# Router logits computed beside the attention products instead of from a transposed second LayerNorm, with a new order of work around them

## What is computed

```python
# x [8,256,512], ctx [8,256,512], mask [8,256], g_* are two scalars
h = layernorm(x)
p = softmax(where(mask, h @ ctx.T / sqrt(512), -1e30))
x = x + tanh(g_xattn) * where(any(mask), p @ ctx, 0)
h = layernorm(x)                                   # [2048, 512]
probs = softmax(h @ w_router.T)                    # 8 experts
top_v, top_i = top_k(probs, 2); top_v /= top_v.sum(-1)
# each row goes through its two experts (inner size 192)
y = sum_k top_v[k] * (silu(h @ gate_k.T) * (h @ up_k.T)) @ down_k.T
x = x + tanh(g_ffn) * y
```

## Time and profile before

| | us |
|---|---|
| median of 3 runs | 261.72 (261.54 to 262.96) |
| the profiled execution | 262.24 |
| its span, first to last instruction | 260.4 |
| PE busy | 242.4 (93%) |
| POOL busy | 166.8 (64%) |
| DVE busy | 164.5 (63%) |
| ACT busy | 146.8 (56%) |

### The profile page before, as it was taken

One profiled execution on the slowest core, in us unless ns is written; L12 is line 12 of the kernel. 1 busy time (PEld: TensorE's weight loads), 2 busy tenths in 40 slices (PEclk: granted clock), 3 DMA queues, 4 the chain that ended last, 5 costly groups with the idle time before them and its releaser, 6 DMA issues.

```text
span 260.4 us, 5397 instructions
## 1 busy us (share of the span) xinstructions
PE 242.4 (93%) x1484; PEld 207.7 (80%) x1484; DVE 164.5 (63%) x618; ACT 146.8 (56%) x307; POOL 166.8 (64%) x165
## 2 busy tenths in 40 slices
PE   1989999999999999998999999999999999999940
PEld 1867778877877778997989998999999999999920
DVE  4559989999997987977855354454454454454420
ACT  3487789988799663533535454454454454454430
POOL 1247889888989647384346654888688665767550
PEclk9999999999999999999999999999999999999985
DMA  6999999999995238376346845899889975987763
GB/s 195 392 390 401 397 371 379 381 345 334 365 399 194 86 102 253 112 149 126 43 59 147 155 91 123 135 166 159 150 162 157 170 137 87 166 156 135 109 79 44
DMA packets 25950, 52.08 MB, mean 200 GB/s; under 512 B 5248, under 2 KB 5376, under 8 KB 25920
## 3 DMA queue, kind: packets, MB, share of 16 engines
q0 software_dynamic: 8304, 19.83, 41.7%
q1 hardware_dynamic: 13008, 23.50, 25.3%
q10 hardware_dynamic: 4608, 8.39, 8.4%
HBM read 33.81 MB, written 17.89 MB: 199 GB/s over the span
## 4 chain that ended last, share of the span: by engine, by line
PE 82%; DMA 5%; issue 4%; SPq 2%; DVE 2%; POOL 2%; ACT 1%; another core or an unknown queue 0%; POOLq 0%; ACTq 0%
PE PO L1217 11%; PE S L1206 9%; PE S L1360 9%; PE S L1364 9%; PE S L1361 9%; PE A L1350 6%; PE PL L1234 5%; PE S L1371 3%; DMA WGl<-in_wgu 3%; PE A L1225 3%; PE A L1188 2%; DMA out<-YT,IXI 2%; PE PO L1384 1%; PE PO L1388 1%; PE A L1384 1%
## 5 line engine op out<-in xcount | busy, mean ns | idle before, releaser
L1360 PE MATMUL S<-WGh,XTh 128*128 x144 | 51.2, 355 | 0.1
L1361 PE MATMUL S<-WGl,XTh 128*128 x144 | 48.3, 336 | 0.0
L464 POOL DMA_INDIRECT XG<-x2s,IXG x30 | 29.5, 983 | 17.1 <-issue 6.8
L634 ACT ACTIVATE SG<-S 128x192 f32<-128x192 f32 x36 | 11.9, 331 | 48.6 <-PE S L1364 48.6
L531 POOL DMA_INDIRECT out<-YT,IXI x19 | 30.3, 1595 | 12.5 <-issue 7.7
L1092 DVE TENSOR_TENSOR H<-SG,S 128x192 f32<-128x192 f32 x36 | 12.7, 354 | 37.6 <-ACT SG L634 35.0
L422 POOL TENSOR_TENSOR rs<-mv,CS 128x1 f32<-128x1 f32 x32 | 19.4, 606 | 22.6 <-DVE mv L749 22.3
L1217 PE MATMUL PO<-CX,PT 128*128 128x512 f32 x64 | 31.3, 611 | 0.2 <-ACT PT L582 0.2
L1364 PE MATMUL S<-WGh,XTl 128*128 x144 | 30.9, 336 | 0.0
L1206 PE MATMUL S<-CT,XLT 128*128 128x256 f32 x128 | 30.3, 379 | 0.0
L1085 DVE TENSOR_TENSOR XTl<-A,XTh 128x512 fp32r<-128x512 f32 x37 | 25.5, 690 | 7.4 <-ACT XTh L627 6.5
(11 more groups left out here) (189 smaller groups left out, 556.1 us busy)
## 6 DMA issues: line engine op xcount, KB each, us to landing
WGl<-in_wgu SPq DMA_DIRECT2D x24, 256.0 KB, 6.4
X<-in_x SPq DMA_DIRECT2D x16, 256.0 KB, 5.7
CT<-in_ctxt SPq DMA_DIRECT2D x8, 512.0 KB, 6.5
CX<-in_ctxn SPq DMA_DIRECT2D x8, 512.0 KB, 6.0
out<-X ACTq DMA_DIRECT2D x16, 256.0 KB, 5.6
x2s<-Y ACTq DMA_DIRECT2D x16, 256.0 KB, 5.3
WD1l<-in_wd SPq DMA_DIRECT2D x8, 256.0 KB, 6.2
WS<-in_wd SPq DMA_DIRECT2D x6, 256.0 KB, 5.8
```

The costliest lines, as they stand in the source:

```text
L464: pool.indirect_dma_start(out=XG[:, xg(j), :], out_offset=None, in_=rows, in_offset=bass.IndirectOffsetOnAxis(ap=at, axis=0))\
L1360: pe.matmul(o, XTh[:, j % 2, c, :], WGh[:, bass.ds(e, 1), c, :], start=(c == 0), stop=False)
L1361: pe.matmul(o, XTh[:, j % 2, c, :], WGl[:, bass.ds(e, 1), c, :], start=False, stop=False)
```

## The change

The logits of the second LayerNorm are no longer computed from its transpose. With centred router weights WRc (each expert's weights less their mean over the channels, `centre`), the logit of a row is its second reciprocal root times (x + attention output) · WRc, and a common positive factor doesn't change which experts are largest. So:

- CT gets 8 more columns that hold WR (loaded with the context), and `score` runs over 264 columns (CC) instead of 256. The 8 columns are the logits of the centred input tile. `rowmax` copies them, scaled, to LG (one DVE instruction more per tile).
- `cw(b, c)`, new on PE, multiplies one half of a batch's transposed context with WRc into PL: 4 products of 8 columns per step, in place of `rt`. `cwe(b)`, new on ACT, copies the result behind the context in CX (now 520 columns wide), once per batch.
- `pv` runs in two pairs: 256 columns into PO and 264 into A1. PO and A1 are now one two-bank tensor PP. `x2` gets one more DVE instruction, which adds 1/sum times the 8 extra columns to LG; the old one reads both banks.
- `t2`, `rt` and `ev2` are gone, and with them Y2T.
- `top2` reads LG, and runs two steps sooner; `odd(b)`, new, takes the difference of the two largest logits times the reciprocal root (two DVE instructions per batch, where batches 5 to 7 had one), before `weigh`, which gets one exponential fewer. `slots`, `cum`, `tab` come one step sooner, `coefs` one later; `st1` stands behind `rowmax`.
- PE's order in a step: t1, score, tp, cw, pv instead of t1, tp, score, rt, pv, t2. `first_list` stands in step 15 ahead of `pv(13)`.
- The end of the attention and SIDES are written anew: `slots(4)` and `top2(6)` now lie inside the steps, `tp(15)` and `tx(0)` ahead of `pv(15)`, the first two gathers ahead of `second(13)`, `store_x2(15)` behind `silu(0)`. In tiles 0 to 3 PE has tab(4), cum(5); tab(5), cum(6); tab(6), cum(7).

```diff
-SIDES = [(4, 6, 6), (4, 5, 4), (2, 3, 5), (2, 2, 3), (2, 2, 2), (0, 2, 3), (2, 3, 5), (2, 1, 2)] + [(0, 0, 0)] * 31
+SIDES = [(3, 6, 6), (3, 5, 4), (2, 3, 3), (5, 1, 2), (0, 5, 0), (1, 4, 4), (0, 1, 3), (3, 3, 2), (0, 0, 0), (0, 0, 0)] + [(0, 0, 0)] * 29
...
+            def centre():
+                dve.wait_ge(s_gb, 1)
+                n = mark(dve.reduce_sum(wm[:, :], PC[:, 16:48].rearrange("p (k e) -> p e k", e=E), AX.X))
+                yield
+                need(n)
+                dve.scalar_tensor_tensor(out=WRc[:, :, :], in0=wm[:, :].unsqueeze(1).to_broadcast([128, KC, E]),
+                                         scalar=-1.0 / D, in1=WR[:, :, :], op0=ALU.mult, op1=ALU.add).then_inc(s_wrc, 1)
+                yield
...
                 n = mark(dve.reduce_max(nmx[:, k:k + 1], SC[k % 2][:, 0:S], AX.X, negate=True))
                 yield
+                logit[k] = mark(dve.tensor_scalar(LG[:, k, :], SC[k % 2][:, S:CC], 1.0 / SCALE, None, ALU.mult))
+                yield
...
-                dve.scalar_tensor_tensor(out=xt, in0=PO[:, :], scalar=rinv[:, k:k + 1], in1=xt,
+                need(logit[k])
+                logit[k] = mark(dve.scalar_tensor_tensor(out=LG[:, k, :], in0=A1[:, S:CC], scalar=rinv[:, k:k + 1],
+                                                         in1=LG[:, k, :], op0=ALU.mult, op1=ALU.add))
+                dve.scalar_tensor_tensor(out=xh, in0=PP[:, :, 0:S], scalar=rinv[:, k:k + 1], in1=xh,
                                          op0=ALU.mult, op1=ALU.add).then_inc(s_x2, 1)
...
+            def odd(b):
+                dve.wait_ge(s_rs2, 2 * b + 2)
+                dve.wait_ge(s_lc, b + 1)
+                if b:
+                    dve.wait_ge(s_e2, b)
+                for i in range(2):
+                    n = dve.scalar_tensor_tensor(out=dd[:, i, :], in0=mx[:, i, 1:2], scalar=mx[:, i, 0:1],
+                                                 in1=rs2[:, 2 * b + i:2 * b + i + 1], op0=ALU.subtract, op1=ALU.mult)
+                n.then_inc(s_dd, 1)
+                yield
...
-                if s + 2 < NTK:
+                if s < 3:
                     main.append(st1(s + 2))
                 if 0 <= s - 1 < NTK:
                     main.append(rowmax(s - 1))
+                if 3 <= s < NTK - 2:
+                    main.append(st1(s + 2))
...
-                if s >= 6 and s % 2 == 0:
-                    side.append(top2((s - 6) // 2))
-                if s >= 8 and s % 2 == 0 and s < NTK:
-                    side.append(slots((s - 8) // 2))
-                    side.append(coefs((s - 8) // 2))
+                if s >= 5 and s % 2 == 1:
+                    side.append(odd((s - 5) // 2))
+                if s >= 4 and s % 2 == 0:
+                    side.append(top2((s - 4) // 2))
+                if s >= 9 and s % 2 == 1:
+                    side.append(coefs((s - 9) // 2))
+                if s >= 7 and s % 2 == 1:
+                    side.append(slots((s - 7) // 2))
...
+                if k % 2 == 0:
+                    pe.wait_ge(s_cwe, b + 1)
                 for c in range(2):
-                    m = pe.matmul(PO[:, :], PT[:, k % 2, c, :], CX[:, b % 2, c, :], start=(c == 0), stop=(c == 1))
+                    pe.matmul(PO[:, 0:S], PT[:, k % 2, c, :], CX[:, b % 2, c, 0:S], start=(c == 0), stop=(c == 1))
+                    m = pe.matmul(A1[:, 0:CC], PT[:, k % 2, c, :], CX[:, b % 2, c, S:DW], start=(c == 0), stop=(c == 1))
                 m.then_inc(s_pv, 1)
...
+            def cw(b, c):
+                if c == 0:
+                    pe.wait_ge(s_ct[b % 2], 16 * (b // 2 + 1))
...
+                for q in range(KC):
+                    m = pe.matmul(PL[:, 8 * c:8 * c + 8], CT[:, b % 2, q, 128 * c:128 * c + 128], WRc[:, q, :],
+                                  start=(q == 0), stop=(q == KC - 1))
```

296 lines of the change are left out of this document (138 added, 158 removed).

## The result

The changed kernel takes 274.43 us, the median of 4 runs (273.33 to 276.44), against 261.99 for the kernel before in the same session. The ratio is 1.048, 95% interval 1.041 to 1.055: slower by 12.4 us. Forecast was 258.7, with a range up to 262.0. The profiled execution has 274.1 us and a span of 272.2.

A forecast was written before the change was run, and what follows sets the result against it. Attention was taken as PE-bound with DVE just behind, DVE then taking over. +0.2 us at the first expert product and −3.2 behind it turn the profiled 262.24 into 259.2; the median, 0.5 lower, is 258.7, range 254.8 to 262.0.

The forecast's parts named there:

- PE's sum: PE's attention step of 5.54 us: t2 −0.44, score +0.05, pv +0.03, together −0.36 per step, −4.7 for 13.
- I add 0.2 for a later start: Start of attention: cwe and centre lie mostly in PE's idle time in steps 1 and 2, costing 0.2 us.
- A tile of lag is not lost at once: Attention steps: pv(s−2) needs only x2(s−3), leaving DVE about 2.4 us of play per PE step.
- The sum of DVE's time: First to fourteenth x2: 72.8 − 3.6 − 1.0 + 7.0 = 75.2 us, 74.2 to 76.4 by the bounds.
- the cover of evp was misjudged: Sign before pv: if PE waits for ACT's PT instead of DVE's X, cw's 0.79 us does not cover evp's 0.7.
- The price of the small instructions: 38 small DVE instructions added between the two x2: 0.10 us each, +3.8; bounds 0 and 0.16.
- Casts at 1.2 us: Sign of rival 3: DVE's 10 weight-unit casts go from a mean of 0.83 to 1.2 us, +3.7.
- rival 3: DVE clearly overloaded, slower: fourteenth x2 at 99.7, first expert product at 107.5, 265.4 us in all; chance 0.11.
- The hand-over: Fourteenth x2 to first expert product: 7.8 us instead of 10.3, first product at 101.5, 0.2 later than before.
- −3.2: First expert product to th(7): 2.5 us of t2 and rt gone, 0.7 of a stall; −2.0 to −4.2.
- there each PE instruction less counts in full: Expert part: PE is alone, tiles every 3.91 us, DVE idle more than half the time from 139 us on.
- a wait of PE for gather(4): Expert part, sign of a rival where DVE paces and the stall stays: gather(4) late by 0 to 1.5 us; chance 0.21.

The follow-up runs named there:

- e9: Changed kernel with only the start-up reordered: router weights loaded earlier, centring earlier, batch 0's weighted context behind the first score; 272.61 us, ratio 1.038.
- e2: Changed kernel with DVE's own subtractions of steps 7 and 9 given to POOL and those of 8 and 10 to DVE; 271.37 us, ratio 1.031.
- e7: Changed kernel with the transposes of P ahead of the score on PE again, as in the kernel before; 275.43 us, ratio 1.052.
- e1: Changed kernel with evp ahead of the store of x2 and of weigh in ACT's queue; 274.38 us, ratio 1.045.
- e5: Changed kernel with the edits of e1, e2 and e3 together; 269.11 us, ratio 1.029.
- e12: Kernel before with two more small DVE instructions per batch tile of attention, their output unused; 263.67 us, ratio 1.003.
- e3: Changed kernel with the four small DVE instructions for POOL's scatter turns braided with slots(5) instead of behind slots(6); 275.42 us, no ratio.
- e15: e10 with 8 bytes more ahead of the x tiles in SBUF; 266.87 us, a single time, no ratio.
- e17: e10 with context load ahead of weight units, slots(4) behind the fourteenth x2, four list products behind transposes, 8 bytes more in SBUF; 262.33 us, ratio 1.007.
- e4: Changed kernel where the first score no longer waits for the load of the router's weights; 274.61 us, ratio 1.047.
- e8: Changed kernel with the edits of e1 and e3, and eight of DVE's ten weight casts on ACT, their subtractions on POOL; 267.06 us, ratio 1.020.
- e10: e8 with e9's start-up, against the changed kernel; 265.57 us, ratio 1.012.

## Why the prediction was wrong

**PE's sum was right.** 5.18 us a step was forecast, 5.19 to 5.20 came in the steps without a wait or a count product, with cw at 0.79 and no line for t2. But "I add 0.2 for a later start (cwe and centre in steps 1 and 2 lie mostly in idle time)" failed: 3.4 us. The column sums of WR come into the queue ahead of t1(2), score(0) waits for their load (1.45 us), and 24 passes of cw (12 products) stand ahead of pv(0), 2.6 us in the trace after. I had counted none of these, and had looked at PE's idle time before 18 us without laying the new products into it. e9 got 1.5 us of it back; 1.9 stayed, with those passes still ahead of pv(0).

**"A tile of lag is not lost at once ... that leaves DVE about 2.4 us of play in a step of PE".** This step failed, and it is most of the 4.8 us. The sum of DVE's time was right: 75.2 us forecast, and 80.03 less its 4.7 us of waits is 75.4. (Of the 3.6 us of waits that it started from, 0.7 lie ahead of the first x2; with 3.0 its sum is 75.8.) What was missing is those waits: the prediction had used up the ones of before and put none in their place, and that is the 4.8 us. The error was to let an average over 13 steps decide. I had seen that "the steps come out uneven", and summed them. But x2(k+1) needs pv(k+1), pv(k+1) needs x2(k), and between two x2 lie at least the end of one, pv's 1.85 us and the semaphores. A step of 8.0 us on DVE is therefore lost at once to the extent that it exceeds PE's 5.2 and the little play, and the next, lighter step can't give it back, since DVE then waits for pv: 5.57 and 6.03 us passed where DVE was busy for 4.48. e2 shows it with the total all but unchanged (0.8 us less): two subtractions of 0.69 us each (1.73 and 1.26 where they met POOL) out of the odd steps are worth 4.5 us. A second term stood at nothing: the clock. pv(6) and pv(8) ran at 1.2 GHz behind PE's waits, 1.2 and 1.7 us longer than pv(5), and 3.7 of DVE's 4.7 us of waits lie in these two steps and right behind them. In e2, where the clock stayed at 2.4 GHz from the first to the fourteenth x2, the stretch took 75.57 us, close to the 75.25 forecast. How much the clock took and how much the heavy steps by themselves, no run separates; in this trace the clock fell only behind waits that such steps had caused.

**"If PE waits before pv for PT of ACT instead of X of DVE, the cover of evp was misjudged."** PE did so, and the sentence is wrong. e7 gave evp its old cover and the waits stayed; e1 gave evp its own place and they became waits for X. ACT's queue has the store of x2 ahead of evp, so a late x2 always shows as a late PT. I had counted what evp needs from PE and not what stands ahead of it on ACT. e5, set against e2, also shows that this order, although on the chain in each wait, costs nothing as long as DVE is late anyway.

**The price of the small instructions** was too high rather than too low: e12 shows 0.045 each where 0.10 was put, in the kernel before, and nothing of the 0.16. "Casts at 1.2 us", which rival 3 needed, did not come: the casts took 0.42 to 1.00. What came was a subtraction of 1.73 in step 7 instead, which took 0.69 there before (the one in step 9 took 1.50 before and 1.26 after); the earlier trace rows had shown the same effect on casts, and I had left it to the rival.

**The hand-over**, 7.8 us forecast, took 8.28, and the first product came at 109.94 in place of 101.5, 8.0 of the 8.4 us from before. That it came so near is in part luck: the path did not run over rowmax(15) and exp, but over pv(14), which waited 2.26 us for PT and then took 3.4 us at the lower clock, x2(14) and pv(15).

**The expert part.** Of "−3.2" up to th(7) 1.05 came. The instructions are gone, but PE's busy time there fell by 1.8 us and not 2.5, and its idle time grew by 0.8. So "there each PE instruction less counts in full" does not hold in tiles 0 to 6: PE waits for H behind DVE's side work (0.7 us twice, 0.8 once before), with one tile of 6.01 and one of 5.70 (5.63 and 5.69 before). Of the rival "a wait of PE for gather(4)" nothing came: gather(4) started at 116.31, 6.4 us behind the first product. And a wait that I had not looked for did: taken had been moved behind slots(6), and I had costed the order of the side list by DVE's time alone, without asking who waits for each of its results. That is 2.8 us of the expert part (e3); nearly all of it lies behind th(7), where 109.4 was forecast and 113.41 came. The last 0.7 to 0.9 us are the tile's 3.94 in place of 3.91 (e15), which nothing in the trace of before could have shown. And the context, whose load was called nothing beside the rest, came late in nine traces, by 0.2 to 2.1 us, though not in the one of the changed kernel itself.

**The rivals.** Rival 3 had the sign, and its threshold (slower from the point where the fourteenth x2 starts later than 96.7) was passed, at 101.66. But its mechanism holds only in part: it filled DVE to 81 us in all, where 75.4 came; single steps were overloaded and not the whole, and its two prices did not come. I gave it 0.11, because each of its terms was bounded by itself at a mean over all steps.

**What stays open.** Of e17's remaining 0.7% I can name the start (first x2 at 20.07 and 18.25) and the gaps of 6.19 and 7.46 us behind the eleventh x2. How often PE's clock falls in a given execution, what of the 4.8 us it took, and which address sets the tile's 0.03 us, I can't say.

## What to carry to other kernels

Where two engines hand a single buffer to each other, sum the work of the slower one per step and compare the largest step, not the mean, with the other's step; a light step behind a heavy one gives nothing back. When steps of a list are reordered, write beside each who waits for its result on another engine, down to the single number that only tells a queue how to go on. And when a trace says that an engine waits for X, read what stands ahead of X in its queue before you mend X: in e1 and e7 it was mended twice for nothing.

## What the runs showed of the hardware

- The granted clock of TensorE fell from 2.4 to 1.2 GHz behind short idle times: behind 0.59 us of idle and 16 passes of 8 columns (e4, for 3.4 us), behind 1.5 us (the changed kernel at 52.49, whose four pairs of pv passes then took 0.54 to 0.88 us each in place of 0.43 to 0.51), and in e8 it stayed at 0.50 for ten micro-seconds in which PE was busy without a gap. With the slower passes this wait of 1.5 us before pv cost 2.7. Not every such wait was followed by a fall: behind 1.45 us before score(0) of the changed kernel none came. The Trainium skill tells of the clock falling in waits for DMA in "TensorE: Matmul & The Clock Gate", section "HAM oscillation — how this bites in real kernels"; the waits there, some 3 to 5 us, are longer than the ones named here.
- A DVE instruction of 16 columns took 1.16 us beside a subtraction on POOL (e10). There it is the rest of the other engine's instruction that counts and not its own length, so work moved from DVE to POOL can bring some of its cost back to DVE: these small ones took 2.9 us longer in e10 than alone, 1.4 in the changed kernel.
- 8 bytes more ahead of the tiles in SBUF change an fp32r product from 338 to 336 ns at the median (e10, e15) and a tile of experts from 3.94 to 3.91 us.
